# Stacked key and query rows by way of a scratch in DRAM instead of 48 on-chip transfers per batch

## The reference, cut to what matters

```python
x = x + _layernorm(attn(_layernorm(x)))
x = x + _layernorm(ffn(_layernorm(x)))
# attn, per batch and head
kernel1 = softmax(einsum('bhnd,bhmd->bhnm', Q, K_l))
kernel2 = softmax(einsum('bhmd,bhkd->bhmk', Q_l, K_l))
kernel3 = softmax(einsum('bhmd,bhnd->bhmn', Q_l, K))
SV = kernel1 @ iterative_inv(kernel2) @ (kernel3 @ V)
# ffn, per batch: the expert whose autoencoder loses least
losses = mean((relu(x @ Wd1 + bd1) @ Wd2 + bd2 - x) ** 2)
out = x @ W_base + adapter[argmin(losses)](x)
```

## Time and profile before

| what | value |
|---|---|
| median of 3 runs | 2256.9 us (2251.79 to 2258.25) |
| the profiled execution's own time | 2251.81 us |
| its span in the profile | 2250.1 us |
| TensorE busy | 2045.9 us, 91% |
| VectorE busy | 1471.5 us, 65% |
| ScalarE, GpSimd busy | 864.0 us and 701.1 us, 38% and 31% |
| mean granted TensorE clock | 0.987 of full |

### The profile page before, as it was taken

How to read it: one execution, slowest core, us unless ns; L and a number is a source line. 1 busy time by engine, 2 the same in 40 slices (tenths; PEclk the granted TensorE clock), 3 DMA queues, 4 the chain that set the end, 5 groups by cost and what they waited for, 6 DMA issues and landing times.

```text
span 2250.1 us, 59443 instructions
## 1 busy us (share of the span) xinstructions
PE 2045.9 (91%) x25341; PEld 1321.1 (59%) x25341; DVE 1471.5 (65%) x3319; ACT 864.0 (38%) x1509; POOL 701.1 (31%) x916
## 2 busy tenths in 40 slices
PE   4889999999999999999999999999999999999955
PEld 2655657566574756657475565756657475665724
DVE  4667575776757676675766767576675767767541
ACT  3334344343434434343344434334343443434221
POOL 4153142422315232332523224252231524223052
PEclk9999999999999999999999999999999999999978
DMA  6223151331414122151422315132231513213020
GB/s 156 45 54 71 30 130 33 90 63 42 102 30 124 38 80 65 20 133 30 116 47 70 64 30 132 30 100 53 64 80 30 131 32 88 64 35 92 12 57 19
DMA packets 232974, 150.74 MB, mean 67 GB/s; under 512 B 153035, under 2 KB 203732, under 8 KB 232693
## 3 DMA queue, kind: packets, MB, share of 16 engines
q1 hardware_dynamic: 232710, 146.95, 27.7%
HBM read 36.98 MB, written 16.78 MB: 24 GB/s over the span
## 4 chain that ended last, share of the span: by engine, by line
PE 60%; DVE 18%; SPq 8%; issue 4%; ACT 3%; POOL 3%; DMA 2%; DVEq 1%; POOLq 0%; ACTq 0%
PE NS L986 11%; PE ringF L1194 9%; SPq L429 8%; PE ringF L1179 6%; PE KV L1067 5%; PE ringA L1153 5%; PE ringA L880 4%; DVE mx L1541 3%; PE ringF L1227 3%; DVE stage L1631 3%; PE ringA L1053 3%; PE ringA L1029 3%; PE ringF L880 2%; PE ringF L1229 2%; ACT E L690 2%
## 5 line engine op out<-in xcount | busy, mean ns | idle before, releaser
L1194 PE MATMUL ringF<-x,H 128*128 128x256 f16 x1536 | 237.9, 273 | 0.0
L1555 DVE TENSOR_REDUCE mx<-ringA 128x8 f32<-128x512 f32 x256 | 175.6, 686 | 88.4 <-PE ringA L1029 87.9
L682 ACT ACTIVATE E<-ringA,score_scale 128x512 f32<-128x512 f32 x256 | 175.4, 686 | 116.3 <-PE ringA L1053 115.9
L1194 PE MATMUL ringF<-H 128*128 128x128 f16 x1024 | 204.5, 220 | 1.4 <-DVE H L1642 1.4
L1608 DVE SCALAR_TENSOR_TENSOR X<-X,NS 128x320 f32<-128x320 f32 x160 | 78.1, 488 | 179.0 <-PE NS L986 173.8
L516 POOL TENSOR_SCALAR vtmp<-mv,eps_ffn 128x8 f32<-128x8 f32 x16 | 5.0, 316 | 607.7 <-DVE mv L1386 607.7
L880 PE MATMUL ringA<-xT,wqkv 128*128 128x512 f16 x768 | 176.5, 379 | 16.9 <-ACT QS L700 11.7
L1179 PE MATMUL ringF<-wd,x2T 128*128 128x512 f16 x768 | 185.4, 380 | 3.4 <-DVE H L1642 3.2
L690 ACT ACTIVATE E<-ringA,score_scale 128x512 f32<-128x512 f32 x256 | 158.6, 684 | 73.3 <-PE ringA L1084 73.3
L1541 DVE TENSOR_REDUCE mx<-ringA 128x1 f32<-128x512 f32 x256 | 160.2, 683 | 28.6 <-PE ringA L1020 28.6
L516 POOL TENSOR_SCALAR vtmp<-mv,eps_ln 128x8 f32<-128x8 f32 x32 | 9.9, 310 | 516.2 <-DVE mv L1386 516.2
(11 more groups left out here) (263 smaller groups left out, 4425.5 us busy)
## 6 DMA issues: line engine op xcount, KB each, us to landing
KS<-stage SPq DMA_DIRECT2D x384, 64.0 KB, 2.0
QS<-stage SPq DMA_DIRECT2D x384, 64.0 KB, 2.0
xin<-in_L_attn_x_dram SPq DMA_DIRECT2D x16, 1024.0 KB, 10.9
xres<-in_L_attn_x_dram SPq DMA_DIRECT2D x16, 1024.0 KB, 8.0
out_dram<-yout SPq DMA_DIRECT2D x16, 1024.0 KB, 5.5
QS<-LB SPq DMA_DIRECT2D x16, 512.0 KB, 4.4
E<-in_L_attn_w_qkv_dram SPq DMA_DIRECT2D x1, 768.0 KB, 7.2
H<-in_L_ffn_Wd_dram SPq DMA_DIRECT2D x2, 256.0 KB
```

The source lines that it names most:

```text
L682: A(E[:, k % ESLOTS, :], ps[:, :], ACT.Exp, scale=score_scale[:, 0:1]).then_inc(freed["s3"].sem, 1)
L1194: ins = MM(dst, H[:, a, t, own], src, start=first and i == 0, stop=last and i >= 3, skip_group_check=True)
L1555: V_.reduce_max(mx1[:, t, 8 * h:8 * h + 8], take(b, "m1", k)[:, :].rearrange("p (a m) -> p a m", a=8), AX.X)\
```

## The change

Each j is now first written as it stands in `stage` to a scratch in DRAM, one transfer of 512 KB, and then read back from there into the three stacked row groups, three transfers of 256 KB. That is 4 writes and 12 reads per batch. ScalarE refills `stage` when the write of j - 2 is done (`stw`), not when the stacked rows are there. SyncE's order, two places in ScalarE's order, and a count of `keep_warm` change with it.

```diff
-        stk = [sig(f"stack{j}", 12, 16) for j in range(4)]
+        stk = [sig(f"stack{j}", 3, 16) for j in range(4)]
+        stw = [sig(f"stack_written{j}", 1, 16) for j in range(4)]
+        scratch = nc.dram_tensor("stack_rows", [4, P, 2, N], F16, kind="Internal").ap()
...
+            def write_rows(b, js):
+                for j in js:
+                    sp.wait_ge(freed["pk"].sem, freed["pk"].at(b, 2 * j + 2))
+                    sp.sem_inc(s_apart, 1)
+                    sp.dma_start(scratch[j, :, :, :], stage[:, j % 2, :, :]).then_inc(stw[j].sem, 16)
+
+            def read_rows(b, js):
+                for j in js:
+                    sp.wait_ge(stw[j].sem, stw[j].at(b, 1))
+                    sp.sem_inc(s_apart, 1)
+                    S = KS if j < 2 else QS
+                    for a, part in enumerate((0, 1, 0)):
+                        sp.dma_start(S[32 * a:32 * a + 32, 4 * (j % 2):4 * (j % 2) + 4, :],
+                                     scratch[j, :, part, :].rearrange("(q r) n -> r q n", r=32)).then_inc(stk[j].sem, 16)
...
-                for j in range(4):
-                    if j == 2:
-                        if not first(b):
-                            sp.wait_ge(x1_done.sem, x1_done.at(b - 1, 2))
-                            sp.sem_inc(s_apart, 1)
-                    if j == 3:
-                        fold_rows3(b)
-                    sp.wait_ge(freed["pk"].sem, freed["pk"].at(b, 2 * j + 2))
+                write_rows(b, (0, 1))
+                read_rows(b, (0, 1))
+                write_rows(b, (2, 3))
+                if not first(b):
+                    sp.wait_ge(x1_done.sem, x1_done.at(b - 1, 2))
                     sp.sem_inc(s_apart, 1)
-                    S = KS if j < 2 else QS
-                    for q in range(4):
-                        if j == 2 and q == 2 and not first(b):
-                            transposes2(b - 1)
-                        for a, part in enumerate((0, 1, 0)):
-                            sp.dma_start(S[32 * a:32 * a + 32, 4 * (j % 2) + q, :],
-                                         stage[32 * q:32 * q + 32, j % 2, part, :]).then_inc(stk[j].sem, 16)
+                read_rows(b, (2, 3))
+                if not first(b):
+                    transposes2(b - 1)
+                fold_rows3(b)
...
                     if j >= 2:
-                        act.wait_ge(stk[j - 2].sem, stk[j - 2].at(b, 12))
+                        act.wait_ge(stw[j - 2].sem, stw[j - 2].at(b, 1))
...
-                staged(b, (2,))
+                staged(b, (2, 3))
                 if ffn:
                     halves2(b - 1, (0,))
-                staged(b, (3,))
+                values(b, (2,))
                 if ffn:
                     halves2(b - 1, (1,))
-                values(b, (2, 3))
+                values(b, (3,))
...
                     if k == 5:
-                        keep_warm(512, 8)
+                        keep_warm(512, 1)
```

More of the change, by code:

```diff
@@ L1015, in maxima3 @@
                 if k == 0:
-                    pe.wait_ge(stk[0].sem, stk[0].at(b, 12))
+                    pe.wait_ge(stk[0].sem, stk[0].at(b, 3))
                 if p == 4:
-                    pe.wait_ge(stk[1].sem, stk[1].at(b, 12))
+                    pe.wait_ge(stk[1].sem, stk[1].at(b, 3))
                 ps = get(b, "m3", k)
@@ L1024, in maxima1 @@
                 if t == 0:
-                    pe.wait_ge(stk[2 + h].sem, stk[2 + h].at(b, 12))
+                    pe.wait_ge(stk[2 + h].sem, stk[2 + h].at(b, 3))
                 ps = get(b, "m1", k)
```

## The result

The changed kernel is slower, and by far more than forecast: 2359.1 us median of five runs (2351.3 to 2372.0) against 2251.8 us before (2248.2 to 2258.3, the three runs of the table above and two more), ratio 1.0475 with an interval of 1.0441 to 1.0508. The profiled execution of it took 2371.96 us and is the slowest of the five. The direction was forecast; the size, 107 us where 22 stood, lies outside the range.

A forecast was written before the change was run, and what follows sets the result against it. TensorE bounds, busy 91%, except one stretch per batch where SyncE issues the keys' 24 transfers. 15 x (0.75 transposes' wait + 0.9 clock) - 2.1 for batch 0 = +22.7 us on 2251.81: 2274, range 2232 to 2302.

The forecast's parts named there:

- the transposes' wait: TensorE's first `hidden` of a batch waits for `x2T`, queued behind the reads, and starts 0.75 us later than before.
- The keys' rows: Rows of j = 0, written to DRAM and read back, arrive at 840.4, 0.4 us later than before, at no cost.
- D: End of VectorE's low halves of j = 3 in a batch: 847.3 in place of 849.40, 2.1 us earlier.
- The clock: TensorE's wait before `hidden` halves its clock in about half of all batches: 0.9 us per batch, bounds 0 and 1.7.
- Batch 0: The first batch, without feed-forward or transposes, keeps its gain of 2.1 us.
- the place: Each batch's start, where SyncE needs 16.33 us to issue 24 transfers of the keys.
- The transposes' issue: SyncE issues the transposes after the last three reads, at 852.0, 1.8 us later than before.
- The much slower rival: DRAM takes 1.2 us more for the keys' write and read-back, clock lost in most batches: 2309 us; chance 0.15.
- "same" case: `hidden` starts at 856.6 to 857.3 and the clock does not fall: 2245 to 2256 us; chance 0.17.

The follow-up runs named there:

- prices: The changed kernel with separate groups of reads and one write added behind its last store; three reads into 32 partitions took 5.74 us, six 9.35.
- half_queue: The changed kernel with the transposes issued between the reads of j = 2 and those of j = 3; 2306.2 us, 1.0240 of before.
- ports: The changed kernel with five groups of 256 KB reads into different partitions behind its last store; eight into 0 to 63 took 13.6 us, into 32 to 95 9.6.
- t_first: The changed kernel with the transposes issued ahead of the reads of j = 2 and j = 3; 2299.7 us, 1.0205 of before.
- early_reads: The changed kernel with the reads of j = 2, then the transposes, issued ahead of the write of j = 3; 2242.9 us, 0.9960 of before.
- only_input: The changed kernel with the next input's load moved from ahead of the keys' writes to behind the write of j = 2; 2334.5 us, 1.0362 of before.
- warm_hole: The changed kernel with 28 matmuls on constants in TensorE's wait before the batch's first `hidden`; 2339.2 us, 1.0387 of before.

## Why the prediction was wrong, point by point

**The step that failed is the transposes' wait, by the rate of the reads ahead of them.** The prediction said that the reads' data, "2.0 us after the issue and 2.1 long, fill the DMA engines from 852.3 to 854.5". That these data stand ahead of the transposes was right; their length was not. The prediction took the rate from a load of 1 MB into 128 partitions that moved in 2.7 us, some 390 GB/s, and it counted the reads of j = 3 alone, as if those of j = 2 were through. Measured, each read takes 1.2 us (prices; 1.2 us apart in the batch above), so the reads of j = 2 are not through when those of j = 3 are issued, and all six lie ahead. In the mean their last packet came 5.8 us after the transposes' issue, not 2.5, and `hidden` 3.1 us after that packet, where 3.4 stood. From issue to `hidden` it is 8.9 us in the mean where the forecast had 5.7: 3.2 us per batch. half_queue, prices and ports show the rate, t_first and early_reads that the reads' place makes the wait.

**The keys' rows were mis-sized too.** D was to come 17.6 us after the first write and came at 19.6: 0.1 us gained where 2.1 stood. In the mean of batches 1 to 14 the write landed after 6.1 us behind the load (forecast 5.85), and the reads of j = 0 took 6.2 (forecast 4.8). So maximum 0 came after 12.5 us, later than the 11.5 (841.2) at which the forecast said it would begin to cost, and, at 842.2 on the clock of that batch, past the 842 that it had named as a sign of being wrong. Most of what was missed is the rate of the reads again. With the load out of the way the rows are nearly in time, and 25 us come back in all (only_input). The two terms make the first `hidden` 5.9 us later than before, not 0.75.

**The clock** cost about 1.3 us per batch (warm_hole) where 0.9 stood: the mechanism was right, but every batch paid and not half of them. The Trainium skill ("TensorE: Matmul & The Clock Gate", "HAM oscillation"), which I had quoted, tells of a clock that falls in each step: the trace agrees, with half clock behind all 15 waits. The 1.7 us that I had put on each batch by it is as far from 1.3 as my 0.9.

**Batch 0** was to keep a gain of 2.1 us. Its D did come 2.2 us earlier, but the batch lasted 128.7 us against 127.5: in it TensorE was at half clock for 30.7 us, 17.0 before. What lowered it was not tried.

The sum: per batch 2.0 for D, 3.2 for the way from issue to `hidden`, and 1.1 for what is lost behind it (a batch lasts 141.0 us against 133.1, and 5.9 of the 7.9 lie ahead of `hidden`), makes 6.3 us over the forecast. Fifteen of them and 3.4 for batch 0 on top of 2274 give 2372, as profiled. The other runs are 11 to 21 us faster than the profiled one, so this is an account of that execution.

**Right** were the place, the mechanism and the direction, and that D gains 2.1 us when the keys are not held up. The transposes' issue, 4.66 us after D where 4.7 stood, was right with some luck: in the kernel the write landed after 3.0 us (forecast 2.85), and issuing the last three reads took 1.5 us (forecast 1.75). Alone, the write took 2.72 us. The estimate of 3.2 us by the Trainium skill ("DMA: Bandwidth & Descriptors", "Anatomy of one DMA") comes from a section on transfers issued from GpSimd; for this write on SyncE's queue the measurement decides. That freshly written DRAM costs nothing extra was assumed, and prices bears it out. The much slower rival named part of what happened (the keys late, the clock lost), but for a slow DRAM, which prices does not show. Its middle, 2309, is still 50 us short. The upper end of the "same" case should read 2254, not 2256 (15 x 0.3 less 2.1 on 2251.81); nothing hangs on it.

## What to carry to other kernels

Fewer, larger transfers take the issue time off the path, but on a shared queue they turn it into bytes that stand ahead of every later transfer: for each, list what is issued ahead of it and multiply by the rate of that very shape, measured, not by that of another. Where the same bytes must move, place each transfer by when its reader comes; here order alone spans 2233 to 2359 us. Take the rate of a read from the partitions that it fills.

## What the runs showed of the hardware

Eight reads of 256 KB into 64 partitions ran at 188 or at 268 GB/s, by whether the second half of the partitions was 32 to 63 or 64 to 95 (ports). Eight reads into 128 partitions averaged 254 GB/s from the first to the last packet, with slices of up to 400, where the 1 MB load of the earlier trace rows averaged 280, with 370 in its full slices; what makes the reads sag is open. Reads of rows written a moment before were no slower than others (prices). A transpose behind six reads of 256 KB moved its first packet 4.6 us after its issue, behind three 2.9, behind none 1.2 (the change, half_queue, early_reads). In four batches of the change the first transpose ran beside a fetch of instructions and took 5.0 to 5.2 us from its first packet to its landing, in the others 3.3 to 4.6; that was not taken apart.
